# Attention in three stages: scores for the maxima issued ahead of those for the exponentials, and two split VectorE pairs

## The reference, cut to what matters

```python
x = x + _L0_attn_a_ref(_layernorm(x), ...)   # causal, relative position bias   (stage A0)
x = x + _L0_ffn_ref(_layernorm(x), ...)      # recurrent
x = x + _L0_attn_b_ref(_layernorm(x), ...)   # a state-space scan
x = x + _L0_ffn_ref(_layernorm(x), ...)
x = x + _L1_attn_a_ref(_layernorm(x), ...)   # not causal                       (stage A1)
x = x + _L1_ffn_ref(_layernorm(x), ...)      # eight experts, top 2
x = x + _L1_attn_b_ref(_layernorm(x), ...)   # causal, rotary                   (stage B1)
x = x + _L1_ffn_ref(_layernorm(x), ...)

# the core of each attention
scores = einsum('bhqd,bhkd->bhqk', q, k) / sqrt(8)      # + bias, + causal mask
out    = einsum('bhqk,bhkd->bhqd', softmax(scores), v)  # then @ WO
```

## Time and profile before

| | us |
|---|---|
| median of three runs | 5572.13 |
| the profiled execution: its own time | 5531.82 |
| its span | 5529.6 |
| TensorE busy in the span | 4268.0 (77%) |
| VectorE busy | 3617.1 (65%) |
| ScalarE busy | 2857.4 (52%) |
| mean granted TensorE clock | 0.904 |

### The profile page before, as it was taken

The page is one execution under the profiler, slowest core; times in us unless marked ns, Lnnn a source line. Parts: engine busy times, 40 slices in busy tenths (PEclk is TensorE's granted clock), DMA queues, the critical chain, the costliest instruction groups (busy, mean ns, idle before and its releaser), DMA issues. The chain is left out here.

```text
span 5529.6 us, 110801 instructions
## 1 busy us (share of the span) xinstructions
PE 4268.0 (77%) x31637; PEld 2118.3 (38%) x31638; DVE 3617.1 (65%) x8801; ACT 2857.4 (52%) x5331; POOL 1613.7 (29%) x1559
## 2 busy tenths in 40 slices
PE   6499999987576766778868889853987588885498
PEld 3144444542122222226312222233973233333397
DVE  2488888546699999984279999950115688885012
ACT  7255555664455555556547777731323366663132
POOL 3000000010577777751200000055534100005552
PEclk9699999997799999999669999976998799997699
DMA  7522222003200000000532222213654333331366
GB/s 246 145 76 70 69 75 70 25 22 137 89 25 25 25 25 28 33 13 2 186 96 74 71 77 72 76 52 114 212 176 156 123 92 91 92 90 54 123 212 191
DMA packets 546189, 501.98 MB, mean 91 GB/s; under 512 B 163774, under 2 KB 482911, under 8 KB 545788
## 3 DMA queue, kind: packets, MB, share of 16 engines
q1 hardware_dynamic: 527724, 460.95, 28.0%
q0 software_dynamic: 18160, 37.42, 2.0%
HBM read 330.57 MB, written 167.58 MB: 90 GB/s over the span
## 5 line engine op out<-in xcount | busy, mean ns | idle before, releaser
L1412 ACT ACTIVATE p_probs<-p_t_ps 128x512 f32<-128x512 f32 (+1 forms) x2304 | 1141.8, 551 | 716.6 <-PE p_t_ps L1303 274.8
L1933 PE MATMUL p_y_ps<-p_prod,c_ident 128*128 128x512 f32 x1024 | 550.1, 663 | 307.8 <-DVE p_prod L2116 306.9
L1316 PE MATMUL p_o_ps<-p_probs,p_v_st 128*32 128x256 f32 (+3 forms) x8704 | 726.7, 407 | 2.9 <-ACT p_o_sb L1398 2.9
L2065 POOL TENSOR_TENSOR p_dbx<-p_dtx,p_b_sb 128x512 f32<-128x512 f32 x512 | 642.6, 1279 | 253.2 <-ACT p_b_sb L1964 245.4
L1237 POOL TENSOR_TENSOR p_v_st<-p_v_raw,p_ones 128x128 f32<-128x128 f32 x192 | 87.7, 457 | 2145.8 <-PE p_o_ps L1316 2022.5
L1449 DVE TENSOR_REDUCE p_row_max<-p_s_ps 128x1 f32<-128x512 f32 x1072 | 659.0, 681 | 81.6 <-PE p_s_ps L1254 43.5
L2107 DVE TENSOR_TENSOR_SCAN p_state<-p_da,p_dbx 128x512 f32<-128x512 f32 x512 | 597.7, 1205 | 74.4 <-ACT p_da L2002 54.1
L1285 PE MATMUL p_t_ps<-p_t_q,p_t_k 50*128 50x512 bf16 (+3 forms) x3072 | 516.0, 336 | 164.1 <-ACT p_probs L1412 65.2
L1254 PE MATMUL p_s_ps<-p_s_k,p_s_q 48*128 48x512 bf16 (+3 forms) x3216 | 508.1, 340 | 164.7 <-DMA p_s_k<-stack_k 66.3
L1446 DVE CUSTOM_DVE_ANT_0 p_tried<-p_s_ps,p_s_bias 128x512 bf16<-128x512 f32 (+3 forms) x1072 | 471.5, 487 | 120.2 <-PE p_s_ps L1254 95.8
L1446 DVE CUSTOM_DVE_ANT_0 p_tried<-p_s_ps,c_mask_row 128x512 bf16<-128x512 f32 (+3 forms) x1072 | 469.0, 488 | 104.4 <-PE p_s_ps L1254 49.4
(11 more groups left out here) (254 smaller groups left out, 7017.1 us busy)
## 6 DMA issues: line engine op xcount, KB each, us to landing
p_wb<-in_w SPq DMA_DIRECT2D x142, 512.0 KB, 3.7
p_s_q<-stack_q SPq DMA_DIRECT2D x408, 96.0 KB, 2.2
p_s_k<-stack_k SPq DMA_DIRECT2D x408, 96.0 KB, 2.3
p_t_q<-stack_q SPq DMA_DIRECT2D x390, 96.0 KB
p_t_k<-stack_k SPq DMA_DIRECT2D x390, 96.0 KB
mamba_inputs<-p_out SPq DMA_DIRECT2D x17, 1536.0 KB, 5.6
p_inp<-mamba_inputs SPq DMA_DIRECT2D x17, 1536.0 KB, 6.7
stack_q<-p_parts SPq DMA_DIRECT2D x51, 384.0 KB, 2.6
```

What stands on the lines that cost most here:

```text
L1316: mm = pe.matmul(o_ps[32 * j:32 * j + 32, at:to], v_st[:, g % 2, c, j, :], probs[:, g % 2, j, place[c] + at - first:place[c] + to - first] ...
L1412: act.activation(exps, tile, ACT.Exp, scale=scale).then_inc(expd, 1)
L1933: pe.matmul(y_ps[:, h], w["ident"], prod[:, k_slot(n, h, RS)], start=(n == 0), stop=(n == STATE - 1)).then_inc(acc_mm, 1)
L2065: pool.tensor_tensor(dbx[:, k_slot(n, h)], dtx[:, u, h], b_sb[:, n % RB], ALU.mult).then_inc(dbx_ready, 1)
```

## The change

In `step`, TensorE now issues `scores_s` of a tile ahead of `scores_t` of the same tile, and VectorE takes `maxima` ahead of `add_bias` (A0 only). VectorE's two split pairs are pulled apart: the shift's high part stays where it was and its rest comes after the next tile's maxima; the reciprocal of the sums and the multiplication likewise. The second instruction raises `misc_read` itself, and the waits for its own completion are gone. For this OT moves from tile 2 to 3 and WO from 4 to 5 in the causal stages, and WO from 5 to 6 in A1. `store_m` waits for `misc_read`, and BT's own wait for the division is covered by `use`.

```diff
-        misc_at = dict(MT=1, OT=2, WO=4, BT=5)
+        misc_at = dict(MT=1, OT=3, WO=5, BT=5)
...
-        misc_at = dict(MT=1, OT=3, WO=5, BT=7)
+        misc_at = dict(MT=1, OT=3, WO=6, BT=7)
...
-            def store_m(b, k):
+            def store_m(no, b, k):
                 bb, g = spread(b, k)
-                sp.wait_ge(shift_ready, 2 * (4 * bb + g) + 2)
+                sp.wait_ge(misc_read, no + 1)
...
                     at = NTILE * pair + i
+                    scores_s(b, v, g + AHEAD, pair, i)
                     scores_t(b, v, g, pair, i)
-                    scores_s(b, v, g + AHEAD, pair, i)
...
                 dve.tensor_scalar(shift[:, g % 2, 0], misc[0:16, 0:P], -1.0, None, ALU.mult).then_inc(shift_ready, 1)
-                dve.wait_ge(shift_ready, 2 * n + 1)
+
+            def shift_low(b, k):
+
+                bb, g = spread(b, k)
+                dve.wait_ge(shift_ready, 4 * bb + g + 1)
                 dve.scalar_tensor_tensor(shift[:, g % 2, 1], misc[0:16, 0:P], -1.0, shift[:, g % 2, 0],
-                                         ALU.mult, ALU.subtract).then_inc(shift_ready, 1)
-                dve.wait_ge(shift_ready, 2 * n + 2)
-                dve.sem_inc(misc_read, 1)
+                                         ALU.mult, ALU.subtract).then_inc(misc_read, 1)
+
+            def sums_inverted(no):
+                dve.wait_ge(misc_mm, no + 1)
+                dve.reciprocal(inv[:, :, :], by_head(misc)[:, :, :, DK]).then_inc(inverted, 1)
+
+            def divide(b, k):
...
+                dve.wait_ge(inverted, n + 1)
+                dve.tensor_tensor(o_n[:, :, 4 * g:4 * g + 4, :], by_head(misc)[:, :, :, 0:DK],
                                   inv[:, :, :].unsqueeze(3).to_broadcast([P, 4, 4, DK]), ALU.mult
-                                  ).then_inc(divided, 1)
-                dve.wait_ge(divided, 2 * n + 2)
-                dve.sem_inc(misc_read, 1)
+                                  ).then_inc(misc_read, 1)
...
                     at = NTILE * pair + i
+                    maxima(b, v, g + AHEAD, pair, i)
                     if i in ADDED:
                         add_bias(b, v, g, pair, i)
-                    maxima(b, v, g + AHEAD, pair, i)
                     if at == misc_at["MT"]:
-                        shifts(use_no(b, g, "MT"), b, g + 2)
+                        shift_high(use_no(b, g, "MT"), b, g + 2)
+                    if at == misc_at["MT"] + 1:
+                        shift_low(b, g + 2)
                     if at == misc_at["OT"] and started >= 2:
-                        divide(use_no(b, g, "OT"), b, g - 2) if g >= 2 else divide(use_no(b, g, "OT"), b - 1, g + 2)
+                        sums_inverted(use_no(b, g, "OT"))
+                    if at == misc_at["OT"] + 1 and started >= 2:
+                        divide(b, g - 2) if g >= 2 else divide(b - 1, g + 2)
```

More of the change, by code:

```diff
@@ L1133, in attend @@
         shift_ready = ph.sem("shift_ready")
-        divided = ph.sem("divided")
+        inverted = ph.sem("inverted")
         block = ph.block()
@@ L1192, in _ @@
                 load_s(0, k)
-            store_m(0, 0)
-            store_m(0, 1)
+            store_m(0, 0, 0)
+            store_m(1, 0, 1)
             sp.wait_ge(zeroed, 3)
@@ L1205, in step @@
                 load_t(b, g + 1)
-                store_m(b, g + 2)
+                store_m(use_no(b, g, "MT"), b, g + 2)
             for g in range(4):
@@ L1338, in ot, with bt @@
                 mm.then_inc(misc_mm, 1)
-            def bt(no, b):
+            def bt(no):
                 use(no)
-                pe.wait_ge(divided, 2 * (4 * b + 3) + 2)
                 for c in range(4):
@@ L1371, in step @@
                     if at == misc_at["BT"] and g == 1 and started >= 4:
-                        bt(use_no(b, g, "BT"), b - 1)
+                        bt(use_no(b, g, "BT"))
             for g in range(4):
@@ L1385, in _ @@
             ot(last + 1, NB - 1, 3)
-            bt(last + 2, NB - 1)
+            bt(last + 2)
             wo(last + 3)
@@ L1463, in add_bias, with shift_high @@
                                       ).then_inc(biased, 1)
-            def shifts(no, b, k):
+            def shift_high(no, b, k):
                 bb, g = spread(b, k)
@@ L1472, in shifts, with by_head @@
                 dve.tensor_scalar(shift[:, g % 2, 0], misc[0:16, 0:P], -1.0, None, ALU.mult).then_inc(shift_ready, 1)
-                dve.wait_ge(shift_ready, 2 * n + 1)
+            def shift_low(b, k):
+                bb, g = spread(b, k)
+                dve.wait_ge(shift_ready, 4 * bb + g + 1)
                 dve.scalar_tensor_tensor(shift[:, g % 2, 1], misc[0:16, 0:P], -1.0, shift[:, g % 2, 0],
-                                         ALU.mult, ALU.subtract).then_inc(shift_ready, 1)
-                dve.wait_ge(shift_ready, 2 * n + 2)
-                dve.sem_inc(misc_read, 1)
-            def divide(no, b, k):
-                n, g = 4 * b + k, k % 4
-                view = misc[:, :].rearrange("p (c j d) -> p c j d", c=4, j=4)
-                dve.wait_ge(misc_mm, no + 1)
-                dve.reciprocal(inv[:, :, :], view[:, :, :, DK]).then_inc(divided, 1)
-                dve.wait_ge(divided, 2 * n + 1)
-                dve.tensor_tensor(o_n[:, :, 4 * g:4 * g + 4, :], view[:, :, :, 0:DK],
+                                         ALU.mult, ALU.subtract).then_inc(misc_read, 1)
[3 more added lines that the diff above has]
+            def divide(b, k):
+                n, g = 4 * b + k, k % 4
+                dve.wait_ge(inverted, n + 1)
+                dve.tensor_tensor(o_n[:, :, 4 * g:4 * g + 4, :], by_head(misc)[:, :, :, 0:DK],
                                   inv[:, :, :].unsqueeze(3).to_broadcast([P, 4, 4, DK]), ALU.mult
-                                  ).then_inc(divided, 1)
-                dve.wait_ge(divided, 2 * n + 2)
-                dve.sem_inc(misc_read, 1)
+                                  ).then_inc(misc_read, 1)
+            def by_head(bank):
+                return bank[:, :].rearrange("p (c j d) -> p c j d", c=4, j=4)
             def gather(no):
@@ L1504, in _ @@
                 if k:
-                    shifts(k - 1, 0, k - 1)
+                    shift_high(k - 1, 0, k - 1)
+                    shift_low(0, k - 1)
             def step(b, v, g):
@@ L1529, in _ @@
             last = use_no(NB, 0, "MT")
-            divide(last, NB - 1, 2)
-            divide(last + 1, NB - 1, 3)
+            for k in (2, 3):
+                sums_inverted(last + k - 2)
+                divide(NB - 1, k)
             gather(last + 2)
```

## The result

The changed kernel's median was 5602.4 us (five runs, 5597.7 to 5613.6), against 5568.5 us for the kernel before (five runs, 5550.6 to 5575.2). The ratio is 1.0072, with a 95% interval of 1.0049 to 1.0095: slower, by 27 to 53 us. In a second measurement on another chip it was 1.0091 (1.0059 to 1.0122). The forecast was 5594 us, +22 us, in a range of 5563 to 5630.

The account below looks back on a forecast made before the run. It took TensorE and VectorE, nearly level, to bound A0 and B1 through waits on each other, and VectorE to bound A1. 64 - 32 - 10 = +22 us on 5572 gave 5594 us, range 5563 to 5630.

Parts of the forecast that it names:

- The sign and the mechanism in A0: A0: tile 1's `scores_t` waits for maxima and then bias, so a plain step takes 12.77 us against 11.78.
- the chain: A0 step head: hand-over 0.57, maxima 1.33 and 0.75 after the bias starts, 2.65 us from `scores_s` to tile 1's `scores_t`.
- the steps with BT and WO: Steps where these jobs move VectorE's wait behind the next tile 0; their extra was left as it was.
- What the splits are worth in A0: A0: VectorE's saving from the split pairs counts for nothing, since it waits for TensorE.
- the sum "+64 us": A0: 1.0 us longer per step, 64 times; bounds +45 and +80.
- -32 forecast: B1: 8.68 us per step against 9.23, taken as -0.5 per step, -32 us; bounds -55 and -5.
- -10 forecast: A1: VectorE saves 0.8 us and loses 0.6 to new waits per step, -10 us; bounds -35 and +5.
- The new wait for MT: A1: MT comes later, behind `pv` and tile 1's `scores_t`, so VectorE waits 0.2 us for it.
- Rival (3): All three stages: the split saves nothing, +30 in B1, +30 in A1, +64 in A0, 5696 us; chance 0.06.
- Rival (2): A0: the bias comes in time, A0 keeps 11.8 us a step, total 5530 us; chance 0.13.
- Rival (1): A0's loss of 45 cancels B1's and A1's gains, about 5573 us; chance 0.19 together with rival (4), nothing of substance moves.
- The store's later start: `store_m` waits for the shift's rest, about 1 us later; costed at nothing, else TensorE would wait for shift rows.

Follow-up runs that it names:

- order_only: The kernel before with only the two issue orders exchanged, pairs unsplit and small jobs unmoved; 5740.2 us against 5555.5, one profiled execution each.
- filler: The changed kernel with tile 0's two `scores_t` matmuls in A0 each issued three times more, same result; timed 1.0039 of the kernel before.
- moved_only: The kernel before with only the small jobs OT and WO moved, pairs unsplit, old issue order; 5553.4 us against 5556.2, profiled.
- split_only: The changed kernel with both issue orders put back, split pairs and moved small jobs kept; timed 0.9839 of the kernel before.
- after: The changed kernel itself, against the kernel before: new orders, split pairs, moved small jobs; median 5602.4 us, ratio 1.0072.
- divide_joined: split_only with reciprocal and multiplication behind each other again, the multiplication raising `misc_read` itself; profiled A0 764.6, A1 751.0, B1 570.9 us.

## Why the prediction was right, and where it was not

**The sign and the mechanism in A0: right.** Tile 0's `scores_s` to tile 1's `scores_t` 2.56 us, forecast 2.65; the plain step without a clock drop 12.76, forecast 12.77; VectorE idle 1.07 us ahead of tile 3, forecast about 1. With the clock held up the stage's change is +65.5 us, forecast +64.

That the numbers meet so closely is in part luck. TensorE's own step is shorter than the chain, 635.24 - 622.61 = 12.63 us, and the second plain step takes 12.51, below the 12.6 to 12.9 forecast; while the steps with BT and WO, whose extra was left as it was, cost 0.33 us more per round of four over the plain ones than before. The two cancel: a round without clock drops is 3.93 us longer than the 48.67 before, forecast four times 0.99. TensorE's marked empty time in a plain step rose by 0.8 us (0.93 to 1.73), where 1.0 was said.

**What the splits are worth in A0: wrong.** The prediction put them at nothing here, since VectorE waits for TensorE, and charged the 1.0 us a step to the new order. But order_only is 147 us longer than the kernel before, and splits and moved jobs together take 48 of it back: the order costs about 2 us in a plain step (13.81 and 13.58 against 11.78 and 11.69), and the rest of the change returns 1.05. The sum came out since the chain was drawn for the whole changed kernel, with OT behind tile 3 and no idle behind the pairs.

**The size of A0: wrong by a missing term.** The step that failed is the sum "+64 us" with bounds of +45 and +80, which held TensorE's matmul lengths as they were. Measured is +98.7. Behind the empty time at the head of the step, 0.66 and 0.82 us with 0.4 us of matmuls between, the clock fell 24 times, and with filler in the first piece the drops and 33 us were gone (all but one drop). The forecast saw the empty time and did not ask what it does to the clock. None of its rivals had this either.

**B1: mechanism right, -32 forecast, -27.3 measured.** (The forecast's terms add up to 0.55 us a step, 35 us for 64 steps; it was rounded to 0.5.) The plain step that it used went from 9.23 to 8.66 us, forecast 8.68. The other plain step gained less, 9.14 to 8.78, and so did those with BT and WO, 9.70 to 9.25 and 10.11 to 9.78, whose extra the forecast left as it was: 1.71 us in a round of four, 27 in 16 rounds. The experiments (moved_only, split_only, after, each against the one ahead of it) divide it into 15 us lost by the moved jobs, 48 gained by the splits and 6 lost by the new order; the forecast had 1.0 us a step gained by the splits, 64 us, and 0.46 lost to new idle, so both of its terms were too large and the errors went opposite ways.

**A1: -10 forecast, -14.6 measured.** The new wait for MT was there (0.22 to 0.33 us in front of the shift, forecast 0.2). The plain steps take 10.89 and 11.18 us, forecast about 11.0. By split_only, the order took back 18 us of a gain of 32.

**Rival (3), the split saves nothing,** would have put the total at 5696. It is excluded: B1 fell instead of rising by 30, and gained 48 us by the split over moved_only. The Trainium skill, "VectorE: DVE Perf Modes", section "The DRAIN you can't avoid", says from a row of copies that a semaphore between operations costs nothing extra. That does not carry over to an engine that waits on a semaphore for its own last instruction, 0.39 and 0.37 us of idle each time. For the wait inside the pair, which divide_joined kept, the trace agrees: nothing in A0 and at most 3 us in A1.

**Rival (2),** faster since the bias would come in time, is excluded by the 2.56 us. **Rival (1),** the terms cancel, is excluded by both intervals. The store's later start cost nothing visible: no wait for the shift rows shows among TensorE's waits in the middle of any of the three stages.

The total landed in the range, and nearer than it deserved: the stage sum is 35 us above the forecast, the timed median only 8 us. Part of that is that the kernel before measured 5568.5 us in five runs instead of the 5572.1 of three, and part that the timed difference, 34 us, was smaller than the 57 us of the profiled stages; in the second measurement it was about 51, by the ratio.

## What to carry to other kernels

When two engines hand tiles to each other in two interleaved streams, look at which stream the long job waits for and try that one first on both engines; in this kernel exchanging the order on one engine only was worse than on both (A0 935.5 and 952.7 against 881.6 us), and on neither was best (764.2). A wait of an engine for its own instruction, only to signal another engine, is replaced by letting the instruction signal: with the halves of the pairs pulled apart this was worth 30 and 48 us in two stages, and for the division the distance by itself gave at most 3 us and cost 15 in B1. Where a change leaves TensorE empty again and again at one place, matmul times read at the higher clock may no longer hold there.

## What the runs showed of the hardware that was not expected

- TensorE's granted clock fell from 2.4 to 1.2 GHz 24 times in A0, each time behind two empty pieces with a few matmuls between them, 22 times of 0.66 and 0.82 us or more; yet most steps with the same pieces kept the clock. With six more matmuls in the first piece it stayed at 2.4 GHz, but for one drop in one of two executions. One empty piece of over 0.3 us a step, of 0.52 to 0.85 us in the middle of the stage in the kernel before and of up to 1.03 us in split_only, did not bring it down. order_only has two such pairs of pieces in each plain step (0.43 and 0.82, 0.66 and 0.82 us) and only 16 drops, so the empty time alone does not say how often it falls. Extra matmuls with no use made the kernel faster, by about 33 us in A0.
- 12 bias matmuls of 384 columns took 1.14 us at the higher level and 1.85 at a mix of both.
- From the start of two 512-column matmuls to the start of a waiting VectorE instruction it was 0.57 us before and 0.59 after (635.24 to 635.83).
